# Top-2 mixture of experts: from all experts on all tokens to tokens sorted by expert through DRAM

## The reference

```python
def _L2_ffn_ref(x, router_w, w13, w2):
    E, H, I, K = (8, 128, 256, 2)
    logits = jnp.einsum('bsh,eh->bse', x, router_w)
    probs = jax.nn.softmax(logits, axis=-1)
    weights, indices = jax.lax.top_k(probs, K)
    weights = weights / (weights.sum(axis=-1, keepdims=True) + 1e-06)
    h13 = jnp.einsum('bsh,ehi->bsei', x, w13)
    gate, up = jnp.split(h13, 2, axis=-1)
    h = jax.nn.silu(gate) * up
    y = jnp.einsum('bsei,eih->bseh', h, w2)
    y_sel = jnp.take_along_axis(y, indices[..., None], axis=2)
    return (y_sel * weights[..., None]).sum(axis=2)
...
x = _layernorm(x + _L2_attn_ref(x, ...), axis=-1)
x = _layernorm(x + _L2_ffn_ref(x, L2_ffn_router_w, L2_ffn_w13, L2_ffn_w2), axis=-1)
```

## Time and profile before

| what | us |
|---|---|
| runs: lowest, median, highest | 2636.87, 2644.38, 2651.82 |
| profiled execution, first to last instruction (its span) | 2628.1 |
| norm and mixture, start to the next stage's start, in that span | 1312.0 to 1638.2 |
| PE busy over the span | 2322.3 (88%) |
| DVE busy | 1851.4 (70%) |
| ACT busy | 1430.5 (54%) |
| POOL busy | 1004.3 (38%) |

### The profile page before, as it was taken

One profiled execution on the slowest core, in us unless ns is written; L12 is line 12 of the kernel. 1 busy time (PEld: TensorE's weight loads), 2 busy tenths in 40 slices (PEclk: granted clock), 3 DMA queues, 4 the chain that ended last, 5 costly groups with the idle time before them and its releaser, 6 DMA issues. The chain is left out here.

```text
span 2628.1 us, 34742 instructions
## 1 busy us (share of the span) xinstructions
PE 2322.3 (88%) x12026; PEld 1723.2 (66%) x12026; DVE 1851.4 (70%) x3430; ACT 1430.5 (54%) x3023; POOL 1004.3 (38%) x791
## 2 busy tenths in 40 slices
PE   7686778898999999999989998688888886999998
PEld 3464556686899999899867777233333333677776
DVE  5667556676666666666577776488888886877776
ACT  6231232697544444444365554566666653877787
POOL 4000000210322222222125556589898985222222
PEclk8698899999999999999989999899999998999999
DMA  4000000000000000000011122223332330011112
GB/s 185 0 1 0 1 1 1 1 1 17 1 1 1 1 1 1 1 1 1 9 58 54 61 61 61 69 81 87 84 86 80 88 82 27 19 45 47 46 45 61
DMA packets 47551, 96.46 MB, mean 37 GB/s; under 512 B 5120, under 2 KB 9232, under 8 KB 46864
## 3 DMA queue, kind: packets, MB, share of 16 engines
q1 hardware_dynamic: 47344, 94.22, 11.9%
q0 software_dynamic: 32, 0.02, 0.1%
HBM read 91.34 MB, written 2.88 MB: 36 GB/s over the span
## 5 line engine op out<-in xcount | busy, mean ns | idle before, releaser
L194 PE MATMUL ps<-TMPr 128*128 128x512 f32 (+4 forms) x3840 | 956.4, 401 | 86.2 <-DVE TMP L210 26.5
L194 PEld LDWEIGHTS ps<-TMPr 128*128 128x128 f32 (+3 forms) x3840 | 718.2, 190 | 322.6 <-issue 77.6
L214 POOL TENSOR_TENSOR TMP<-TMP 128x512 f32<-128x512 f32 (+2 forms) x496 | 639.3, 1311 | 645.2 <-ACT TMP L205 463.4
L194 PE MATMUL ps<-TMP 128*128 128x65 f32 (+5 forms) x4352 | 514.2, 286 | 9.8 <-DVE TMP L213 7.8
L194 PEld LDWEIGHTS ps<-TMP 128*128 128x128 f32 (+3 forms) x4352 | 472.0, 191 | 62.5 <-issue 32.8
L205 ACT ACTIVATE TMP<-ps,W 128x256 f32<-128x256 f32 (+2 forms) x528 | 283.5, 584 | 303.2 <-DVE TMP L210 184.1
L194 PE MATMUL ps<-TMP,W 128*128 128x512 f32 (+5 forms) x720 | 367.8, 634 | 52.7 <-POOL TMP L214 14.7
L210 DVE TENSOR_TENSOR TMP<-ps,TMP 128x512 f32<-128x512 f32 (+1 forms) x434 | 252.5, 603 | 108.4 <-PE ps L194 48.8
L205 ACT ACTIVATE TMPr<-ps,W 128x512 fp32r<-128x512 f32 x352 | 242.9, 690 | 91.9 <-PE ps L194 72.1
L214 POOL TENSOR_TENSOR XT<-XT,XK 128x512 f32<-128x512 f32 x128 | 175.9, 1374 | 293.1 <-DVE XK L213 274.8
L194 PEld LDWEIGHTS ps<-TMP,W 128*128 128x128 f32 (+3 forms) x720 | 124.4, 191 | 220.4 <-issue 155.3
(11 more groups left out here) (188 smaller groups left out, 2523.5 us busy)
## 6 DMA issues: line engine op xcount, KB each, us to landing
TMP<-rows SPq DMA_DIRECT2D x168, 256.0 KB, 3.5
TMP<-gates SPq DMA_DIRECT2D x112, 256.0 KB, 3.3
W<-wp SPq DMA_DIRECT2D x1, 4124.0 KB, 13.6
W<-wp SPq DMA_DIRECT2D x1, 3072.0 KB, 26.4
W<-wp SPq DMA_DIRECT2D x1, 2136.5 KB, 19.7
XT<-xT SPq DMA_DIRECT2D x4, 512.0 KB, 7.5
out<-XK SPq DMA_DIRECT2D x8, 256.0 KB, 2.3
W<-wp SPq DMA_DIRECT2D x1, 1993.0 KB, 15.4
```

What stands on the lines that cost most here:

```text
L194: return nc.tensor.matmul(out, lhsT, rhs, start=start, stop=stop, **k)
L214: gtt = lambda o, a, b, op: nc.gpsimd.tensor_tensor(o, a, b, op)
```

## The change

Stage 6 is written anew, and the norm in front of it becomes part of it. Instead of all experts on all tokens, each token's row goes to the two experts that it chose.

*Dispatch.* Per chunk the norm, the transposes and the logits as before; then `gates` finds the two experts of each token on DVE, PE counts with triangular and all-ones matrices how many tokens ahead of each chose the same expert (`rank`), and `slots` makes of it a row number in an array in DRAM, `sorted`, in which each expert has room for 4096 rows. POOL sends the rows of 144 values (128 features, 8 gate weights, 8 target rows) there with indirect transfers, 128 rows each, two for each 128 tokens. `tiles` computes from the counts which expert each of 72 tiles of 128 rows belongs to, and where its rows lie. Twelve steps split all experts' weights; before, each expert's were split during the previous expert's work.

*Walk.* 72 tiles are always worked on, in pairs. SP loads a tile's rows from an address in a register, eight tiles ahead. PE turns them, multiplies them with the expert's weights, read at an address in a register (three products of 512 columns), ACT takes silu, one DVE instruction multiplies gate, up and weight, PE turns the result, and eight products a pair of 256 or 128 columns project down; DVE adds two halves, and POOL sends the 128 rows of each tile to their target rows in `results` with an indirect transfer. Rows that only fill up a tile have zero weights and go to rows that nobody reads.

*Return.* When all have landed, SP loads the two results of each token (16 transfers of 256 KB), DVE adds them and the normed input, PE turns the rows, and ACT writes `XT`.

`sorted` is first filled with padding rows, nine transfers at the kernel's start behind the weights. Constants for the dispatch are loaded in stage 5. The tap weights of stage 7 now wait for the last tile's up products. In stage 8 only the branches for stage 6 are gone.

```diff
+NTL = 72
+XROWS = 8 * T + 8 * 128
+YROWS = 2 * T + NTL * 128
+YR = 6
...
-    LN_ALONE = [k for k in (1, 2, 3, 4, 5, 8) if k <= LAST]
+    LN_ALONE = [k for k in (1, 2, 3, 4, 8) if k <= LAST]
...
     def stage6():
-        return moe_stage(6)
...
+        plan = [("centre", 0), ("centre", 1)]
+        for i in range(NCH + 2):
+            if i < NCH:
+                plan += [("centre", i + 2)] * (i + 2 < NCH) + [("norm", i), ("back", i)]
+            plan += [("route", i - 1)] * (0 <= i - 1 < NCH) + [("rank", i - 2)] * (0 <= i - 2 < NCH)
+        plan += [("tiles", 0)] + [("split", j) for j in range(12)]
+
+        walk = [("turn_x", 0)]
+        for q in range(NP + 2):
+            if q % 2 == 0 and q // 2 + 1 < NG:
+                walk.append(("turn_x", q // 2 + 1))
+            walk += [("up", 2 * q), ("up", 2 * q + 1)] * (q < NP)
+            walk += [("turn_f", q - 1)] * (0 <= q - 1 < NP) + [("down", q - 2)] * (0 <= q - 2 < NP)
...
+        def pe(e):
...
+                elif step == "up":
+                    if a % 8 == 0:
+                        nc.tensor.reg_load(regs, toff[0:1, a:a + 8])
+                        for j in range(8):
+                            place[a + j] = nc.tensor.snap(regs[j], min_val=0, max_val=3584)
+                    v, (h, l) = place[a], xT[a // 4 % 2]
+                    e.wait_ge(*gl.at(a // 4))
+                    if a >= 3:
+                        e.wait_ge(*prod.at(a - 3))
+                    mm(ph[a % 3], tile(h, a % 4), Wuh[:, bass.ds(v, 512)], True, False)
+                    mm(ph[a % 3], tile(h, a % 4), Wul[:, bass.ds(v, 512)], False, False)
+                    mm(ph[a % 3], tile(l, a % 4), Wuh[:, bass.ds(v, 512)], False, True).then_inc(*dt_up(a))
...
+                elif step == "down":
...
+                    for j in range(2):
+                        v, o = place[2 * a + j], py[a % 2][:, 256 * j:256 * j + 256]
+                        mm(o, tile(h, 2 * j), Wda[:, bass.ds(v, 256)], True, False)
+                        mm(o[:, 0:128], tile(l, 2 * j), Wda[:, bass.ds(v, 128)], False, False)
+                        mm(o, tile(h, 2 * j + 1), Wdb[:, bass.ds(v, 256)], False, False)
+                        r = mm(o[:, 0:128], tile(l, 2 * j + 1), Wdb[:, bass.ds(v, 128)], False, True)
+                    r.then_inc(*dn(a))
...
+        def gates(e, i):
...
+            nc.vector.tensor_reduce(q4(mx, i), l3, AX, ALU.max).then_inc(*sig("max"))
+            done("max")
+            tt(p, l3, spread(q4(mx, i), 8), ALU.subtract).then_inc(*sig("shifted"))
+            e.wait_ge(*ex.at(i))
+            nc.vector.tensor_reduce(q4(sm, i), p, AX, ALU.add).then_inc(*sig("sum"))
...
+        def dve(e):
...
+                elif step == "turn_x":
...
+                    minus(xT[a % 2][1], PS[0], xT[a % 2][0]).then_inc(*gl(a))
+                elif step == "up":
+                    e.wait_ge(*silu.at(a))
+                    if a >= 4:
+                        e.wait_ge(*ft.at((a - 4) // 2))
+                    stt(fb[a % 4], sb[a % 3], sel[a // 4 % 2][:, 2 * (a % 4):2 * (a % 4) + 1], ph[a % 3][:, 256:512],
+                        ALU.mult, ALU.mult).then_inc(*prod(a))
...
+                elif step == "down":
+                    o = py[a % 2].rearrange("p (n h k) -> p n k h", n=2, h=2)
+                    e.wait_ge(*dn.at(a))
+                    if a >= YR:
+                        e.wait_ge(*puts(a - YR))
+                    nc.vector.tensor_reduce(g3(yb[a % YR], 2), o, AX, ALU.add).then_inc(*yv(a))
...
+        def pool(e):
+            e.wait_ge(s_pad, 16 * 9)
+            for step, i in plan:
+                if step == "rank":
+                    e.wait_ge(*da.at((i, "scaled")))
+                    e.wait_ge(*db.at((i, "where")))
+                    for c in range(4 * i, 4 * i + 4):
+                        for h in range(2):
+                            nc.gpsimd.indirect_dma_start(
+                                sorted_d, bass.IndirectOffsetOnAxis(ap=IDX[:, 2 * c + h:2 * c + h + 1], axis=0), st3[:, c, :], None,
+                                bounds_check=XROWS - 1, oob_is_err=False).then_inc(s_sent[c % 4], 16)
+            for step, a in walk:
+                if step == "down":
+                    e.wait_ge(*yv.at(a))
+                    e.wait_ge(*gi.at(a // 2))
+                    for j in range(2):
+                        nc.gpsimd.indirect_dma_start(
+                            result_d, bass.IndirectOffsetOnAxis(ap=DI[:, 2 * a + j:2 * a + j + 1], axis=0), tile(yb[a % YR], j), None,
+                            bounds_check=YROWS - 1, oob_is_err=False).then_inc(s_put[a % YR], 16)
+
+        def sync(e):
+            regs = [nc.sync.alloc_register(f"tile_rows{j}") for j in range(8)]
+            e.wait_ge(*tb.at("row"))
+            for s in s_sent:
+                e.wait_ge(s, 16 * 16)
+            for j in range(NTL):
+                if j % 8 == 0:
+                    nc.sync.reg_load(regs, trow[0:1, j:j + 8])
+                    rows = [nc.sync.snap(r, min_val=0, max_val=XROWS - 128) for r in regs]
...
+                nc.sync.dma_start(xg3[:, j % 8, :], sorted_d[bass.ds(rows[j % 8], 128), :]).then_inc(s_rows_in[j % 8], 16)
+            for q in range(NP - YR, NP):
+                e.wait_ge(*puts(q))
...
+            for i in range(NCH):
+                if i >= 3:
+                    e.wait_ge(*zt.at(i - 3))
+                for h in range(2):
+                    nc.sync.dma_start(h4(YB[i % 3])[:, h], back[:, h, 4 * i:4 * i + 4, :]).then_inc(s_back[i % 3], 16)
...
         def sync(e):
-            e.wait_ge(*me_w.at((6, 7, "low")))
+            e.wait_ge(*dt_up.at(NTL - 1))
             nc.sync.dma_start(Wtap, vecs_d[2:3, :].partition_broadcast(128)).then_inc(s_conv, 16)
...
+        for x in range(8):
+            rows = sorted_d[x * T:(x + 1) * T, :].rearrange("(n p) d -> n p d", p=128)
+            nc.sync.dma_start(rows, pad_d.unsqueeze(0).to_broadcast([T // 128, 128, 144])).then_inc(s_pad, 16)
```

More of the change, by code:

```diff
@@ new lines, in stage6 @@
+        walk = [("turn_x", 0)]
[4 more added lines that the diff above has]
+            walk += [("turn_f", q - 1)] * (0 <= q - 1 < NP) + [("down", q - 2)] * (0 <= q - 2 < NP)
+        names_a = "max shifted sum reciprocal probs top pair pair_reciprocal first replaced taken kept scaled in_chunk so_far".split()
+        names_b = "slot masked second both other high_slot low_slot where".split()
@@ new lines, in stage6 @@
+        names_t = "tokens past tiles ends starts bases reached expert chosen offset picked rows row beyond".split()
+        cen, sq, dev, rec, xk, tr, xa = (Sig(sem("dispatch_" + n), CK) for n in
+                                         ("centred", "squares", "deviation", "reciprocal", "normed", "turned", "rows"))
+        lg, ex, rk = (Sig(sem("dispatch_" + n), CK) for n in ("logits", "exp", "ranks"))
+        da, db = (Sig(sem("dispatch_" + n), [(i, x) for i in CK for x in names]) for n, names in (("gates", names_a), ("slots", names_b)))
@@ new lines, in stage6 @@
+        fill, tot, tb = Sig(sem("dispatch_filled"), ("fill",)), Sig(sem("dispatch_total"), ("all",)), Sig(sem("dispatch_tiles"), names_t)
+        wh, wl = (Sig(sem("dispatch_weights_" + n), range(12)) for n in ("high", "low"))
+        gx, gh, gl = (Sig(sem("tile_x_" + n), range(NG)) for n in ("turned", "high", "low"))
+        gp, gs, go, gi = (Sig(sem("tile_row_" + n), range(NG)) for n in ("picked", "selected", "spare", "targets"))
+        silu, prod = (Sig(sem("tile_" + n), range(NTL)) for n in ("silu", "product"))
@@ new lines, in stage6 @@
+        ft, fh, fl = (Sig(sem("tile_f_" + n), range(NP)) for n in ("turned", "high", "low"))
+        dn, yv = (Sig(sem("tile_" + n), range(NP)) for n in ("down", "result"))
+        zs, zx, zt, zc = (Sig(sem("result_" + n), CK) for n in ("summed", "added", "turned", "rows"))
+        YB = [ax(1024) for _ in range(3)]
+        h4 = lambda ap: ap.rearrange("p (h n k) -> p h n k", h=2, n=4)
+        puts = lambda q: (s_put[q % YR], 32 * (q // YR + 1))
+        arrived = lambda j: (s_rows_in[j % 8], 16 * (j // 8 + 1))
@@ new lines, in slots @@
+        def slots(e, i):
+            sig, done = lambda n: db((i, n)), lambda n: e.wait_ge(*db.at((i, n)))
+            k = i % 2
+            s3, h, t = g3(ms[k], 4), top[:, 0:4], top[:, 4:8]
+            ix = IDX[:, 8 * i:8 * i + 8].rearrange("p (c h) -> p c h", h=2)
+            e.wait_ge(*rk.at(i))
+            tt(s3, g3(pk[:, 32 * i:32 * i + 32], 4), e8(first, 4), ALU.add).then_inc(*sig("slot"))
+            done("slot")
+            tt(ms[k], ms[k], M[k], ALU.mult).then_inc(*sig("masked"))
+            done("masked")
+            nc.vector.tensor_reduce(h, s3, AX, ALU.max).then_inc(*sig("second"))
+            nc.vector.tensor_reduce(t, s3, AX, ALU.add).then_inc(*sig("both"))
+            done("both")
+            tt(g3(eq[k], 4), s3, spread(h, 8), ALU.is_equal).then_inc(*sig("other"))
+            copy(ix[:, :, 1], h).then_inc(*sig("high_slot"))
```

(3 more changed lines are left out.)

490 lines of the change are left out of this document (344 added, 146 removed).

## The result

| kernel | us, median (lowest to highest) | runs |
|---|---|---|
| before | 2644.26 (2636.87 to 2651.82) | 4 |
| after | 2575.16 (2571.24 to 2584.94) | 4 |

The ratio is 0.9741, 95% interval 0.9717 to 0.9764: 69 us faster, where 50 were forecast. The profiled execution of the new kernel took 2584.94 us with a span of 2583.1, so only 1.84 us lie outside a span. The kernel before, profiled once more, took 2633.76 us with a span of 2631.9, again 1.9 apart. The "16.3 us above the span" that the prediction kept was therefore not time outside the span: the profiled execution had been a quick one.

What follows compares the result with a forecast made beforehand. PE's dense products were taken to bound the stage. Dispatch 108, walk 136, return 30 and drain 1.6 us sum to 276 against 326.2, 50 us less: kernel time 2594 us, range 2542 to 2670.

Steps and rivals of the forecast that it cites:

- 16.3 us above the span: Distance kept between the profiled span, 2628.1 us, and the median of the runs shown, 2644.4 us.
- What bounded the kernel before: Norm and mixture stretch of 326.2 us: PE bounds it, with 1152 dense products taking 270 us.
- DVE's chain: Dispatch: DVE's small dependent steps take 8.6 us a chunk; with tables and weight splits DVE is through at 87 us.
- Scatter: Dispatch: POOL's 64 indirect transfers at 1.22 us from 20 us on end at 98 us; first product at 108 us.
- Walk: 36 pairs of tiles at 3.7 us, PE's 3.05 plus 0.6 for imperfect overlap: 133 us, and 3 to drain.
- Register addresses: Walk: addresses in registers on PE cost from 0 to about 0.15 us a product.
- PE's clock: Walk: short gaps could drop PE to 1.2 GHz, doubling the products to about 6 us a pair.
- rival 2: Walk: PE's pace decides, about 6 us a pair, kernel 2677 us; chance 0.09 slower, 0.12 for a mild case.
- Indirect price: POOL's cost per indirect transfer of 128 rows, taken as 1.22 us; break-even with the dense form up to 1.92.
- rival 1: Scatter and walk: a dearer indirect transfer, at 2.34 us, makes the kernel 57 us slower, 2701; chance 0.11.
- Return: After the walk: 16 loads at 1.5 us, 24 us, 3 for landing and 3 for the last steps: 30 us.
- Pads, tap weights, later stages: Outside the stage: all costed at nothing, with 0 to 5 us possible for pads and for a low-clock next stage.

Runs made afterwards that it cites:

- Controls: Both kernels profiled again unchanged: the kernel before 2633.76 us (stretch 327.7), the kernel after 2579.21 us (stretch 257.3).
- half_scatter: Kernel after with each row sent only to its first expert, 32 scatters instead of 64: 2588.61 us, first up product 94.1 us into the stretch instead of 117.0.
- rank_early: Kernel after with each chunk's ranks counted one step earlier: 2565.12 us, ratio to before 0.9714, stretch 251.3 us against 257.3 for its control.
- two_again: Kernel after without one of the three up products of each tile: 2568.05 us, ratio to before 0.9697, pair 2.67 us against 2.96.
- const_again: Kernel after with all walk weights at one constant address and no register loads: 2569.29 us, ratio to before 0.9708, pair 2.96 us.
- best: Kernel after with ranks one step earlier, later pad transfers and four result buffers instead of three: 2571.68 us, ratio to before 0.9715, stretch 247.9 us.
- pads_late: Kernel after with the nine pad transfers moved from the kernel's start to SP's queue in stage 5: 2576.07 us, ratio to before 0.9746.
- two_products: Kernel after without one of the three up products, first time, in the disturbed second set: 2596.3 us in one run, pair 3.44 us.

## Why the prediction was right, and where its sum was off

The forecast's mechanism held: the dense products go, a dispatch bound by POOL's issues takes their first part, a walk and a return the rest. The sum was 276 us and the stretch took 255.7.

- **What bounded the kernel before**: right as to the stretch. What stage 2 and the scan gained or lost is a few us at most and open (see Controls).
- **DVE's chain**: the sum was right in part by luck. 8.6 us a chunk was forecast and is 8.56; DVE was to be through at 87 us and was, at 1415.2, 87.0 in. But its own steps take 5.6 us where 5.9 were counted, and its waits 3.0 where 2.7 were. The wait that the sum put between shift and sum, for transposes, copy, table and exp, is two waits: 2.7 us for PE's transposes at the lower clock, ACT's copy and then PE's logits, which the forecast had not counted; and 0.29 for exp, since the 1.28 us table load lies under the logits and DVE's next two steps. By the Trainium skill ("ScalarE: Activation LUTs", What ACT_TABLE_LOAD costs) a drain of some 1.38 us would have come on top; here the exp starts 1.36 us after its load began, 0.08 after it ended, so the trace of the new kernel does not show it either.
- **Scatter**: the term that decides the dispatch, as half_scatter shows. 64 x 1.22 from 20 us on was forecast; it was 83.1 us from 24.0 on. 61 issues at 1.27 and three at 1.80 make that. The middle of the near rows was a fair price. The first issue came 4 us later than forecast, and the issues took 5 us more. The first product came at 117.0 us, not 108.
- **The three long issues** fall in the time of DVE's splits, each with two inputs from SBUF. The Trainium skill, "SBUF — State Buffer", Who interferes with whom, says that DVE instructions with two SBUF inputs contend with GpSimd instructions that read SBUF; the rows agree in time (1.50 us against 0.97), at a cost of 1.6 us in all. In rank_early and half_scatter the scatter lies otherwise against the splits, and the long issues stay with the splits. But an issue 0.6 us behind the first split took 0.97 in after and in rank_early, so not each one is held, and what holds them is in no row.
- **Walk**: the step that failed in size. PE's own work was forecast as 3.05 us a pair and is 2.96; the 0.6 us added for engines that do not overlap perfectly was not there at all, with DVE at 92% of PE. 36 x 0.74 is 27 us. That the deep buffers (tile loads eight ahead, three accumulators, six result buffers) absorb what the fixed order of each engine could have cost is argued, as no run had fewer. Two_again shows that the period follows the fullest engine to 2%, down to DVE's 2.67.
- **Register addresses**: nothing, at the lower end of the 0 to 0.15 us; const_again shows it. **PE's clock**: full in the walk (1.00), at its lower level (0.50) through the scatter and the return, so rival 2 never came near. **Indirect price** (rival 1): 1.27 us, far from the break-even at 1.92.
- **Return**: 23.4 us from SP's first load to the next stage, forecast 27 and the drain. Transfers pace it, as said, and the reuse of the third buffer, which the forecast left out, adds to it: with a fourth it takes 20.6 us (best).
- **Pads, tap weights, later stages**: costed at nothing, with 0 to 5 us each for the pads and for the next stage's start. pads_late gives the pads at most a few us of the median. The scan's start at a lower clock (0.70 to 0.75 granted, 0.77 before) fits the other term, untested. The tap weights had no run of their own.

The errors were +9 on the dispatch, -27 within the walk (its start and drain gave 3 back) and -5 on the return: the stretch came out 20 us below the sum. The 9 us that the dispatch took over its forecast hid part of what the walk took under it.

## What to carry to other kernels

Where several engines run a loop from deep buffers, take the fullest engine's busy time as the period and put the safety margin in the range, not into the forecast; this is one loop's lesson. Indirect transfers are paid by POOL per 128 rows: count them, place their first issue as early as its data allow, and compare their sum with the chain beside them. Compare a stage between its drains when the stages around it vary more than the effect, and keep an unchanged kernel in each set, since a set without it (the second here) could have been taken for an effect.

## What the runs showed of the hardware

- An indirect transfer of 128 rows took POOL 0.97 us and 0.30 to the next, the same for rows of 576 bytes (scatter) and of 512 (results): 1.27 us, in all twelve profiles.
- Expert weights read at a register's address cost PE nothing: 2.960 us a pair of tiles with and without, at 0.23 us a wide product.
- An issue that starts 1.8, 3.7 or 5.5 us into DVE's run of subtractions with two SBUF inputs took 1.50 us instead of 0.97 in all kernels whose scatter reaches that far, whichever of the 64 it was.
- On one chip four profiles in a row showed a walk of 3.44 to 3.60 us a pair instead of 2.96 (two_products 3.44 instead of two_again's 2.67), with waits for which the trace names no end, while the kernel before took its usual time there. The packets of the DMA queues, those that carry instructions among them, took as long as elsewhere. What it was stays open.
